# A selective-scan layer with a mixture of experts: opening in another order, and the experts' slots found in cumulative counts instead of one-hot products

## The reference, cut to what matters

```python
# norm, projection, convolution
xn = x * rsqrt(mean(x * x) + 1e-6) * norm_w
x_branch, gate = split(xn @ W_in.T)
xc = silu(causal_conv(x_branch, conv_w, 4 taps) + conv_b)
dt = soft_clamp(softplus(xc @ W_dt.T + b_dt), 0.001, 0.1)
dA = exp(soft_clamp(dt * A, -8, 8))
# recurrence
h = h * dA_t + dt_t * B_t * x_t          # every 10th step: h *= min(20 / |h|, 1)
y = C_t . h + D * x_t
x = layernorm(x + x + scale * (y * silu(gate)) @ W_out.T)
# experts
probs = softmax(x @ w_router); gate, eidx = top_k(probs, 2); gate /= sum(gate)
pos = cumsum(one_hot(eidx)) - 1          # a token's slot in its expert, in token order
keep = pos < 768
expert_in[e, pos] = x                    # gather into 768 slots per expert
y = sum(gate * (relu(expert_in @ w1 + b1) @ w2 + b2)[e, pos])
out = layernorm(x + y)
```

## Time and profile before

| | |
|---|---|
| median of three runs | 2746.71 us |
| the profiled execution's own time | 2746.24 us |
| its span in the trace | 2744.1 us |
| mean granted TensorE clock | 0.978 |
| busy: PE, DVE, ACT, POOL | 94%, 87%, 81%, 78% |
| first phase's scans end, routing starts | about 2287 us |
| experts' first matmul | 2350.71 us |

### The profile page before, as it was taken

How to read it: one execution, slowest core, us unless ns; L and a number is a source line. 1 busy time by engine, 2 the same in 40 slices (tenths; PEclk the granted TensorE clock), 3 DMA queues, 4 the chain that set the end, 5 groups by cost and what they waited for, 6 DMA issues and landing times. The chain is left out here.

```text
span 2744.1 us, 50515 instructions
## 1 busy us (share of the span) xinstructions
PE 2577.5 (94%) x16744; PEld 2377.2 (87%) x16744; DVE 2376.0 (87%) x3388; ACT 2216.7 (81%) x4949; POOL 2138.6 (78%) x2244
## 2 busy tenths in 40 slices
PE   7999999999999999999999999999999986899992
PEld 6899999999999999999999999999999875677762
DVE  5899999999999999999999999999999997122124
ACT  5899999999999999999999999999999962111113
POOL 4798888988889888898888988889888883434314
PEclk9999999999999999999999999999999997999996
DMA  2122222222222222222222222222222222224227
GB/s 96 57 79 79 78 79 78 79 79 77 80 78 78 79 76 80 78 79 78 76 81 79 78 78 76 81 78 79 78 76 78 74 76 91 67 75 107 61 48 256
DMA packets 145456, 224.97 MB, mean 82 GB/s; under 512 B 37804, under 2 KB 84652, under 8 KB 144044
## 3 DMA queue, kind: packets, MB, share of 16 engines
q1 hardware_dynamic: 124084, 188.96, 22.4%
q0 software_dynamic: 9216, 12.59, 2.6%
q10 hardware_dynamic: 11896, 20.19, 2.1%
HBM read 188.61 MB, written 33.05 MB: 81 GB/s over the span
## 5 line engine op out<-in xcount | busy, mean ns | idle before, releaser
L806 DVE TENSOR_TENSOR_SCAN H<-DA,PM 128x704 f32<-128x704 f32 (+1 forms) x824 | 1297.7, 1595 | 0.0
L1052 POOL TENSOR_TENSOR H<-H,CB 128x640 f32<-128x640 f32 (+1 forms) x824 | 1205.7, 1477 | 114.2 <-DVE H L806 112.6
L519 ACT ACTIVATE DA<-DT,SM 128x160 f32<-128x160 f32 (+1 forms) x3200 | 1069.0, 422 | 1.2
L1091 PE MATMUL YB<-H,ID 128*128 128x160 f32 (+1 forms) x6592 | 1032.9, 308 | 0.2 <-POOL H L1052 0.2
L1091 PEld LDWEIGHTS YB<-H,ID 128*128 128x128 f32 x6592 | 971.6, 191 | 16.4 <-issue 11.2
L774 DVE TENSOR_TENSOR PM<-PM,BB 128x640 f32<-128x640 f32 (+1 forms) x824 | 667.7, 810 | 0.2
L528 ACT ACTIVATE DA<-DA 128x2560 f32<-128x2560 f32 x204 | 473.0, 2319 | 1.7
L968 POOL TENSOR_TENSOR FC<-SN,HALF 128x4 f32<-128x4 f32 x206 | 232.7, 1129 | 42.0 <-DVE SN L813 38.1
L1104 PE MATMUL PAZ<-XN,RB 128*128 128x160 f32 x1648 | 251.3, 306 | 10.0 <-POOL XN L935 8.0
L1114 PEld LDWEIGHTS PAZ<-XB,CD 128*128 128x128 f32 x1664 | 237.5, 188 | 16.8
L1620 POOL DMA_INDIRECT YA<-YS,IG x48 | 75.2, 1566 | 219.7 <-ACT YS L1451 208.1
(11 more groups left out here) (191 smaller groups left out, 2821.3 us busy)
## 6 DMA issues: line engine op xcount, KB each, us to landing
BB<-Bd SPq DMA_DIRECT2D x208, 320.0 KB, 3.4
CB<-Cd SPq DMA_DIRECT2D x206, 320.0 KB, 3.3
W<-in_w ACTq DMA_DIRECT2D x16, 1024.0 KB
XT<-in_xT SPq DMA_DIRECT2D x52, 160.0 KB, 2.2
XR<-in_xp SPq DMA_DIRECT2D x208, 40.0 KB
X2d<-VV SPq DMA_DIRECT2D x208, 40.0 KB
YA<-VV SPq DMA_DIRECT2D x208, 40.0 KB
HI<-YA SPq DMA_DIRECT2D x6, 1024.0 KB, 10.0
```

The lines of the kernel that those rows point to most:

```text
L519: eng.activation(DA[:, c0:c0 + k1, :, a, m, 1:11].rearrange("p c b t -> p b c t"), DT[:, j % 2, a].rearrange("p b (c t) -> p b c t", c=2)[ ...
L806: eng.tensor_tensor_scan(H[:, q % 3, u, 0:n], decays(c, g)[:, u], DBX(u)[:, 0:n], 0.0, ALU.mult, ALU.add).then_inc(s_scan, 1)
L1052: eng.tensor_tensor(h, h, cb, ALU.mult).then_inc(s_hc, 1)
L1091: mm = eng.matmul(yv, ID[:], hv[:, :, :, n, 0:w], start=False, stop=n == 15)
```

## The change

The opening. The 16 tap matrices are all written by DVE, and PE's first convolution waits for all of them. Chunk 3's logarithm is taken straight from PSUM into RST3, a piece of SG that is not yet in use, beside that of chunk 2; its normed x is written by POOL at the end of chunk 0. ACT takes the gate's tanh ahead of the time step's, in chunk 0 and in chunk 1. DVE's `conv_gate(2)` stands ahead of two scans instead of between them. The squares of chunk 4 go from ACT to POOL, and seven of the decay tanhs of chunk 2 stand one place later.

```diff
-        PRE_C, PRE_W, PRE_CV, N_PRE = 9, 13, 21, 25
+        PRE_C, PRE_W, PRE_CV, N_PRE = 9, 13, 29, 33
+        RST3 = SG[:, 1, 0, :, 0:20]
...
             root_log(2, PA[:, 320:480])
+            eng.wait_ge(s_ssum, 4)
+            eng.activation(RST3, YB[1][:, 320:480].rearrange("p (b t) -> p b t", t=20), ACT.Ln,
+                           bias=CST[:, 0:1]).then_inc(s_root, 1)
+            root_exp(2)
+            gate_tanh(0)
             step_tanh(1)
-            root_exp(2)
-            eng.wait_ge(s_ssum, 4)
-            gate_tanh(0)
+            eng.wait_ge(s_root, 4)
+            eng.activation(RST3, RST3, ACT.Exp, scale=-0.5).then_inc(s_rs, 1)
             first_decays(3)
-            mean_out(3, YB[1][:, 320:480])
...
             state_squares(3)
-            step_log(2)
-            eng.wait_ge(s_ms, 1)
-            root_log(3, RST[:])
-            step_tanh(2)
-            root_exp(3)
+            second_tanh(3)
             eng.wait_ge(s_xc, 3)
             gate_tanh(1)
-            second_tanh(3)
+            step_log(2)
+            step_tanh(2)
...
-                for a in (2, 3):
+                for a in range(4):
                     eng.tensor_scalar(CD[:, k, a], ID[:], CW[:, a, k:k + 1], None, ALU.mult).then_inc(s_pre, 1)
...
-            for k in range(4):
-                for a in (0, 1):
-                    eng.tensor_scalar(CD[:, k, a], ID[:], CW[:, a, k:k + 1], 0.0, ALU.mult, ALU.add).then_inc(s_tap, 1)
             x_normed(0)
```

```diff
+            def counted(n):
+                eng.wait_ge(s_grp, n + 1)
+                eng.tensor_copy(RJ[:, 3 * n:3 * n + 3], grp(n)[:, :, 128:130]).then_inc(s_rj, 1)
+                eng.tensor_tensor(LE[:, n // 2 % 2], grp(n)[:, :, 0:128],
+                                  AT[:, 3 * n:3 * n + 3].unsqueeze(2).to_broadcast([128, 3, 128]), ALU.is_le).then_inc(s_le, 1)
+                eng.wait_ge(s_le, n // 2 + 1)
+                eng.tensor_reduce(CN[:, 3 * n:3 * n + 3], LE[:, n // 2 % 2], AX.X, ALU.add).then_inc(s_cnt, 1)
...
+            for n in range(1, 16, 2):
+                eng.wait_ge(s_grp, n + 1)
+                if n > 1:
+                    eng.wait_ge(s_sgn, 4 * (n // 2))
+                for k in range(3):
+                    eng.activation(SGN[:, k], grp(n)[:, k, 0:128], ACT.Sign, bias=HALFWAY[:, 3 * n + k:3 * n + k + 1],
+                                   scale=-1.0, accum_out=CN[:, 3 * n + k:3 * n + k + 1]).then_inc(s_sgn, 1)
+                eng.activation(RJ[:, 3 * n:3 * n + 3], grp(n)[:, :, 128:130], ACT.Copy).then_inc(s_sgn, 1)
...
+            for n in range(16):
+                e = n // 2
+                t, h = e // 2, e % 2
+                eng.wait_ge(s_reach[t], 1)
...
+                for k in range(3):
+                    b = 3 * (n % 2) + k
+                    mm = eng.matmul(grp(n)[:, k, 0:130], REACH[64 * h:64 * h + 64, t, 128 * b:128 * b + 128],
+                                    CU[64 * h:64 * h + 64, t], start=True, stop=True)
+                mm.then_inc(s_grp, 1)
...
+            eng.wait_ge(s_ix, 1)
             load_e(0)
+            eng.wait_ge(s_gd, 16)
+            eng.wait_ge(s_zg, 1)
+            gates(0)
+            eng.wait_ge(s_ix, 2)
             load_e(1)
+            gates(1)
             for e in range(E):
                 load_e(e + 2)
+                gates(e + 2)
```

More of the change, by code:

```diff
@@ L883, in vector_program @@
                         norm_sum(q - 1)
+                    if i == 0 and s == 12:
+                        conv_gate(2, BOTH)
                     if s == 2 and live and i > 0:
@@ L1338, in moe_phase @@
         PB = [ctx.enter_context(nc.psum_tensor(f"PE{i}", [128, 512], F32)) for i in range(8)]
[L1340 to L1344 removed]
+        s_ld, s_ld2, s_lg, s_bl, s_rt, s_ra = sem("ld"), sem("ld2"), sem("lg"), sem("bl"), sem("rt"), sem("ra")
+        s_cum, s_cumc, s_cst, s_ex, s_exc = sem("cum"), sem("cumc"), sem("cst"), sem("ex"), sem("exc")
+        s_reach = [sem(f"reach{t}") for t in range(4)]
+        s_grp, s_le, s_cnt, s_rj, s_sgn, s_idx, s_ix = (
+            sem("grp"), sem("le"), sem("cnt"), sem("rj"), sem("sgn"), sem("idx"), sem("ix"))
+        s_gate, s_wn, s_gd, s_zg, s_last = sem("gate"), sem("wn"), sem("gd"), sem("zg"), sem("last")
+        s_gg = [sem(f"gg{e}") for e in range(E)]
         s_wl = [sem("wl0"), sem("wl1")]
@@ L1532, in vector_program @@
-            eng.tensor_tensor(IG[:, 1], IG[:, 1], IG[:, 0], ALU.add).then_inc(s_rt, 1)
+            logits_less_top(eng, late, s_rt, 1)
+            eng.wait_ge(s_ra, 1)
+            probabilities(eng, late, s_rt, 3)
+            choice(eng, late, 0, s_rt, 6)
+            choice(eng, late, 1, s_rt, 12)
+            both_choices(eng, late, s_rt, 17)
+            eng.tensor_tensor(LAST[:].rearrange("p e (b j) -> p b j e", j=8)[:, 1:8, 0], late.oh[0][:, 0:7], late.oh[1][:, 0:7],
+                              ALU.add).then_inc(s_last, 1)
@@ L1533, in vector_program @@
+            eng.wait_ge(s_ld2, 16)
+            for g in range(2):
+                eng.wait_ge(s_ex, g + 1)
+                eng.tensor_copy(EX[:, 2 * g:2 * g + 2], before(g)).then_inc(s_exc, 1)
+                eng.wait_ge(s_exc, g + 1)
+                reach(2 * g)
+            counted(0)
+            indices(0, 1, 0)
+            for n in range(2, 16, 2):
+                counted(n)
+            indices(1, E, 5)
             eng.wait_ge(s_bl, 32)
```

280 lines of the change are left out of this document (139 added, 141 removed).

## The result

The changed kernel took 2710.07 us (median of 4 runs, 2709.23 to 2711.47) against 2746.7; the ratio is 0.9864 (95% interval 0.9852 to 0.9876). The forecast was 2709.1 us. Its profiled execution took 2710.64 us with a span of 2708.6.

What follows compares the result with a forecast made beforehand. DVE was taken to bound the steady part, with the opening before it and the routing and PE's experts behind. Gains of 32.8 (routing), 2.85 and 1.5 (opening) make 37.15; 2746.24 - 37.15 = 2709.1 us, range 2702 to 2719.5.

Steps and rivals of the forecast that it cites:

- The clock in the search: Routing search on PE: first group 0.7 us longer at the low clock, the rest at full clock, 1.6 us per pair.
- rival (a): Search: clock stays low, 1.5 us per group, 11 us more, 2720.3 us; chance 0.15 together with doubled accumulator cost.
- the cumulated counts: Start of the routing: eight PE matmuls of 128 columns at the low clock, 4.8 us.
- ACT's accumulators: Search: ACT's share per pair between 1.2 and 2.4 us, depending on the accumulator's extra cost; 1.5 taken.
- Routing in all: From DVE's last choice step to the first expert matmul: 23.5 us instead of 56.3, 32.8 us less.
- Expert 0's first layer: First expert matmuls behind the routing: left at their length before, about 21.5 us.
- Opening, first half: Chunk 0: taps on DVE let POOL's XN run from 10.76, PE start at 11.7 instead of 14.54; gain 2.85 us.
- Opening, second half: DVE's waits before it is continuously busy: the longest ends 1.5 us earlier; bounds -1.6 and 1.5 + 2.1.
- full clock in the projection: Chunk 4's projection on PE: upper bound adds 2.1 us of gain; the forecast kept the low clock, 4.47 us.
- The 1.6 us for the scan behind XC: Opening, DVE: XC now stands ahead of two scans, so the scan formerly ahead runs after it; 1.6 us lost.
- POOL's gathers, costed at 0: Expert phase: 48 gathers of gates added on POOL, 26.7 us of PE's 42.67 per expert in all, so 0 added.
- rival (c): Expert phase: POOL becomes the bound, decisive from 4.0 us per gate gather; 2758 us at 5 us; chance 0.02.

Runs made afterwards that it cites:

- e9: The changed kernel run again with nothing altered: 2712.19 us, ratio 0.9871.
- e5: The changed kernel with five matmuls of 384 columns put on PE in its wait ahead of the cumulated counts: 2729.97 us, ratio 0.9931.
- e6: The changed kernel with the 48 search matmuls over all 128 rows instead of 64: 2733.15 us, ratio 0.9941.
- e3: The changed kernel with half of the 16 taps written by POOL ahead of its first normed x again: 2735.4 us, ratio 0.9952.
- e2: The changed kernel with all routing edits undone, so the opening alone: 2741.77 us, ratio 0.9978.
- e12: The changed kernel with e11's parted gathers, e5's five matmuls and e7's order of DVE's copies: 2706.64 us, ratio 0.9847.
- e7: The changed kernel with DVE's copies of expert 0's turned rows ahead of the indices of experts 1 to 7: 2732.06 us, ratio 0.9942.
- e4: The changed kernel with DVE's conv_gate(2) put back between the two scans: 2727.64 us, ratio 0.9926.
- e10: The changed kernel without the 48 gathers of gates, the gates a constant 0.5: 2710.08 us, ratio 0.9861.
- e8: The changed kernel with each of the 48 gathers of gates issued twice: 2771.86 us, ratio 1.0094.
- e11: The kernel of e4 with POOL's gathers parted, their number the same: 2708.64 us, ratio 0.9855.

## Why the prediction was right, step by step

The time (2709.1 against 2710.07 us) was right, and so were the mechanism and the order of what is late. That it is right to 1 us is luck: some terms were mis-sized, and their errors cancelled. Against 37.15 us in all, the opening gave 2.0 more (6.39 instead of 4.35), the routing 1.5 less, expert 0's first layer 1.3 less and the end 0.9 less.

- **The clock in the search.** I let the first group run low and the other fifteen at 1.00. In the first measurement all sixteen ran low. That is rival (a), but not at its price: I had a group at 1.5 us there, and it took 1.02 on average. A pair took 1.90 us instead of 1.6, the first one 2.95, so the search was 2.7 us longer than my 13.5; the cumulated counts, which I had wholly low, ran low at 3.8 us instead of 4.8, at 0.43 us for two records. In e9 the clock was up, and the search took 10.25 us (9.9 busy), less than I had: PE needs less for a group at 1.00 than DVE and ACT do, and a pair goes at their 1.31. ACT's accumulators cost little (its signs of 128 columns start 0.35 us apart, plain activations of 160 columns 0.33), so its share was 1.23, below the 1.5.
- **What moves the clock.** In the first measurement PE was busy for 4.00 of 4.00 us in the search and stayed at 0.50; in e5, with DVE's and ACT's pauses (3.73 of 4.00), it stayed at 1.00; in e6, over 128 rows, it rose. The Trainium skill (TensorE: Matmul & The Clock Gate, "Part 1: The HAM clock gate (the "warmup" mystery)") says that a PE which is kept at work comes up to the full clock: e6 agrees, the search over 64 rows does not. The same page of the Trainium skill says in "A second HAM failure mode: psum-queue depth-cycling" that small pauses between groups make the clock oscillate, and no search here shows that.
- **Routing in all.** 31.27 us in place of 32.8 in the first measurement, and 34.1 in e9.
- **Expert 0's first layer.** I left it at its 21.49 us. It took 22.80: PE came to it at 0.50 (0.72 over 2313 to 2320), as it did in every profile with the new routing. This term was missing from my sum.
- **Opening, first half.** XN was finished at 11.08 and the scaling at 11.63, where I had XN held back until 11.65 and the scaling done at 10.76. The start of PE was right, by the wrong engine. The mis-sized term is the projection behind it: 4.60 us instead of the 3.91 that I took over, so the branch came only 2.07 us earlier in the first measurement; at equal clock it is 3.1 to 3.4 (e3). I had XN wait for both of DVE's scalings. The trace shows the two scalings apart, and the second one was late as well:

```profile
10.28 1.35 DVE L688 TENSOR_SCALAR RB<-RB,SM 128x1024 f32<-128x1024 f32 x1
```

The first one, from 9.62 on, took its usual 0.75 us. XN is recorded from 9.68 with 1.40 instead of 0.85, and the second scaling with 1.35 instead of 0.75: as if XN had waited for the first and the second for XN. The Trainium skill (SBUF — State Buffer, "Who interferes with whom") says of DVE in its two-port mode and POOL that the one that comes first keeps the other out for its whole length. The trace agrees with turns of that kind within 0.2 us; which mode DVE was in no row shows.
- **Opening, second half.** My 1.5 us had a bound of 1.5 + 2.1 "full clock in the projection", and that is what happened in the first measurement: 2.34 us, and 4.0 us gained. In e2, e3, e5 to e9 and e12 it was 4.01 us, and DVE's last wait ended 2.3 to 5.2 us earlier than before with the whole opening in place (e9, e7). The slow projection itself costs 1.2 us (30.44 us from XC of chunk 2 to XC of chunk 3 in e7 and e9, 29.21 in the first measurement); most of the spread comes from the projections of chunks 0 and 1, which my sum left at one length. The 1.6 us for the scan behind XC was right: e4 won back 1.8.
- **POOL's gathers, costed at 0.** Right where there is no stall (0.3 to 2 us, e10), but not for the whole reason. I asked only whether POOL has time enough, and put rival (c) at 4.0 us per gather. e8 became slower than before with POOL far from full. What was missing from my list is a way in which POOL's row of gathers holds up work of others. The trace of before had it already, in expert 0's first layer; I had passed over these rows:

```profile
2362.42 1.00 POOL L1603 DMA_INDIRECT XRE<-X2d,IG  x1 [0.30 <-issue]
...
2364.32 0.58 ACT L1445 ACTIVATE HT<-PE,B 128x384 f32<-128x384 f32 x1 [5.69 <-PE PE L1683]
...
2365.76 1.14 DVE L1552 TENSOR_SCALAR HT<-PE,B 128x384 f32<-128x384 f32 x2 [4.37 <-PE PE L1683]
```

ACT and DVE normally wait 2.00 and 1.96 us there. They were late until POOL's 18 gathers were over, and PE's eight banks hid it. e2, with the routing of before on the chip of e4, has it too, no worse:

```profile
2362.30 0.58 ACT L1454 ACTIVATE HT<-PE,B 128x384 f32<-128x384 f32 x1 [4.27 <-PE PE L1692]
2364.44 1.14 DVE L1561 TENSOR_SCALAR HT<-PE,B 128x384 f32<-128x384 f32 x2 [4.36 <-PE PE L1692]
```

So the forecast held as it was measured, but it has a condition that I did not name: on two of the chips every kernel with the new routing and its unparted gathers (seven of seven) lost 15 us or more behind the last choice step.
- **Two slips in the working.** XN from 10.76 with 0.85 us ends at 11.61, not 11.65, and the three terms named for the lower end of the range, 0.9, 2.1 and 3 us, lead to 2703.1 and not to 2702. Neither changes a conclusion.

**What stays open.** First, what decides whether the row stalls the others. The unparted row ran without a stall only in the unaltered kernel (first measurement and e9), and with one in all seven altered kernels, on two chips on which the unaltered one was never run; e10 to e12 shortened the row or parted it. So chip and program can't be told apart. For the chip speaks that e4 differs from the changed kernel by one instruction of the opening; against it, that the old routing has the same mild stall in the trace of before and in e2, which ran on e4's chip. It is not the engines' spacing alone, for e4 has the first measurement's spacing from its first sign to its first gather (3.82 us in both). If it is the chip, the changed kernel would take about 2730 us there, by e4, e5 and e7; this is an estimate. Second, whether parting the gathers helps there (e11 and e12 were not run there). Third, whether it is PE's signals or the waiting engines that are held up: the late work waited for PE each time, while PE's own waits for DVE and ACT ended on time inside the row (e8: DVE's output ends at 2340.16, PE goes on at 2340.21). Fourth, which clock pattern an execution gets: the mean granted clock of the first series' four executions was 0.978, 0.981, 0.978 and 0.981, so it probably changes on one chip too.

## What to carry to other kernels

Cost a row of indirect DMAs not only by its engine's time but by what waits for other engines beside it, and look in the trace of before for waits that end just when such a row ends. Breaking the row where a chain of short hand-overs runs beside it is worth a trial; that it helps is not shown here. Read PE's clock at the place where a small step begins, not only in the steady part, in more than one execution, and fill a wait ahead of a short chain with matmuls if it begins low. Put the unaltered kernel into every series, on the same chip as its variants, and read the parts from the profiles rather than from the total.

## What was unexpected of the hardware

- Work waiting for PE began up to 19 us late while POOL issued 24 to 54 indirect DMAs in a row at 1.30 us each (waits in e4: ACT 10.02 us, e7: 16.31, e8: 21.13, where 2.00 is usual). On one chip a row longer by 18 gathers made it 23.5 us longer (e8 against e7). The unaltered kernel did not show it with a row of 36.
- Matmuls over 64 rows kept PE busy for 16.25 us at the 1.2 GHz level without a rise in six profiles. They held the 2.4 GHz level in e5, e7, e8, e9 and e12.
- At 0.50 a record of the search (64 rows, 130 columns) came each 0.158 us (a pair of groups, 12 records, in 1.90), one of the counts (128 rows, 128 columns) each 0.215.
- One program showed two clock patterns in different executions: the chunk-4 projection in 2.34 or 4.01 us and PE's busy time in the search 16.2 or 9.9, and the two executions took 2710.64 and 2712.20 us.
- POOL's product of 320 columns and DVE's scaling of 1024, started together, were each recorded longer by 0.55 to 0.60 us, as if they had taken turns.
